# Local attention: inverse norms by ScalarE's logarithm and exponential, and a new order of VectorE's work in a tile

## The reference

```python
qkv = h @ wqkv
q, k, v = jnp.split(qkv, 3, axis=-1)          # 8 heads of 64 each
q = l2norm(q) * qs                            # each head's row divided by its norm
k = l2norm(k) * ksc
q, k = rotary_xpos(q, k)                      # a rotation with position-dependent scales
bk, bv = (look_around(bk), look_around(bv))   # a window's keys and those of the window before
sim = jnp.einsum('bhwid,bhwjd->bhwij', bq, bk)
sim = jnp.where(mask, -jnp.finfo(sim.dtype).max, sim)
attn = jax.nn.softmax(sim, axis=-1)
out = jnp.einsum('bhwij,bhwjd->bhwid', attn, bv)
x = x + o @ wo
```

## Time and profile before

| | us |
|---|---|
| median of 3 runs | 2674.88 (2674.61 to 2675.52) |
| profiled execution | 2674.28 |
| its span, first to last instruction | 2672.5 |
| PE / DVE / ACT / POOL busy | 2413.3 / 2081.4 / 1452.3 / 1173.9 |
| granted TensorE clock, mean | 0.963 of full speed |

### The profile page before, as it was taken

The page is one execution under the profiler, slowest core; times in us unless marked ns, Lnnn a source line. Parts: engine busy times, 40 slices in busy tenths (PEclk is TensorE's granted clock), DMA queues, the critical chain, the costliest instruction groups (busy, mean ns, idle before and its releaser), DMA issues.

```text
span 2672.5 us, 41317 instructions
## 1 busy us (share of the span) xinstructions
PE 2413.3 (90%) x14910; PEld 1127.4 (42%) x14910; DVE 2081.4 (78%) x3341; ACT 1452.3 (54%) x2541; POOL 1173.9 (44%) x980
## 2 busy tenths in 40 slices
PE   6799985988868977887699999999999999999897
PEld 5444434453335654565433333433343334333344
DVE  7798876428879965996588899888889988889642
ACT  5576652627647753675365555455545554555462
POOL 2211110306835531553056666566656665566630
PEclk9899988999989999999899999999999999999999
DMA  5000001010000000000100000000000000000000
GB/s 211 1 1 1 1 1 56 1 44 1 32 16 1 2 32 1 1 1 17 44 1 9 9 9 5 9 9 10 9 9 6 9 9 9 10 9 9 5 1 16
DMA packets 21128, 42.00 MB, mean 16 GB/s; under 512 B 10494, under 2 KB 12670, under 8 KB 19772
## 3 DMA queue, kind: packets, MB, share of 16 engines
q1 hardware_dynamic: 20924, 39.35, 4.3%
HBM read 34.90 MB, written 4.45 MB: 15 GB/s over the span
## 4 chain that ended last, share of the span: by engine, by line
PE 66%; DVE 23%; issue 6%; ACT 3%; POOL 1%; DMA 0%; DVEq 0%; POOLq 0%; ACTq 0%; SPq 0%
PE PS L2672 16%; PE PS L2663 15%; PE PS L1236 6%; PE PS L2635 5%; DVE WK L2188 2%; DVE NR L274 2%; DVE NR L2876 2%; PE PS L1218 2%; DVE WK L2164 2%; PE PS L680 2%; PE PS L682 2%; PE PS L681 2%; DVE WK L271 1%; DVE WK L2171 1%; PE PS L2618 1%
## 5 line engine op out<-in xcount | busy, mean ns | idle before, releaser
L2778 ACT ACTIVATE WK<-PS 128x1024 f32<-128x1024 f32 x512 | 497.6, 1022 | 458.1 <-PE PS L2663 452.4
L2955 POOL TENSOR_TENSOR W<-W,WK 128x512 f32<-128x512 f32 x448 | 575.8, 1287 | 383.4 <-DVE W L2894 382.1
L2876 DVE TENSOR_REDUCE NR<-PS 128x2 f32<-128x1024 f32 x512 | 625.3, 1223 | 131.7 <-PE PS L2636 115.9
L2672 PE MATMUL PS<-WK,W 128*64 128x512 f32 x2048 | 494.1, 603 | 0.0
L2663 PE MATMUL PS<-WK 64*128 64x512 f16 (+1 forms) x4096 | 484.0, 376 | 0.6 <-issue 0.6
L2894 DVE TENSOR_TENSOR W<-W,WK 128x512 f32<-128x512 f32 x448 | 342.8, 767 | 9.9 <-ACT WK L2778 9.4
L2663 PEld LDWEIGHTS PS<-WK 64*128 64x128 f16 (+1 forms) x4096 | 199.2, 94 | 219.8 <-ACT WK L2778 6.5
L2672 PEld LDWEIGHTS PS<-WK,W 128*64 128x64 f32 x2048 | 124.1, 136 | 246.9 <-issue 168.9
L2635 PE MATMUL PS<-WK 64*128 64x512 f16 x512 | 195.4, 382 | 5.5 <-DVE NR L2876 4.9
L2636 PE MATMUL PS<-WK 64*128 64x512 f16 x512 | 195.4, 382 | 0.0
L2203 POOL TENSOR_TENSOR WK<-WK,W 128x512 f32<-128x512 f32 x64 | 113.3, 1792 | 176.1 <-DVE WK L2148 93.8
(11 more groups left out here) (371 smaller groups left out, 4326.7 us busy)
## 6 DMA issues: line engine op xcount, KB each, us to landing
XB<-l_rdens SPq DMA_DIRECT2D x62, 128.0 KB, 2.9
W<-in_mw SPq DMA_DIRECT2D x8, 512.0 KB, 11.8
W<-in_l2w SPq DMA_DIRECT2D x1, 3114.0 KB, 12.0
W<-in_f1w SPq DMA_DIRECT2D x1, 2816.0 KB, 18.6
W<-in_l3w SPq DMA_DIRECT2D x1, 2816.0 KB, 9.9
W<-in_f3w SPq DMA_DIRECT2D x1, 2816.0 KB, 9.8
W<-in_mw SPq DMA_DIRECT2D x8, 256.0 KB, 12.3
la_second_tables<-W SPq DMA_DIRECT2D x1, 2048.0 KB, 6.3
```

What stands on the lines that cost most here:

```text
L2672: m = e.matmul(k.PS[64 * i:64 * i + 64, 4, :], self.V[:, kt, g, :], self.PTB[kt // 2 % 2][:, kt % 2, i, :], start=kt == 0, stop=kt == NT - 1)
L2778: e.activation(self.PTB[kt // 2 % 2][:, kt % 2, :, :], self.k.PS[:, 2 * (kt % 2):2 * (kt % 2) + 2, :], ACT.Exp, scale=1.0 / 64).then_inc(s ...
L2876: e.tensor_reduce(self.PM[ji % 2][:, u // 4, :, u % 4], self.k.PS[:, bk:bk + 2, :], AX.X, ALU.max).then_inc(self.maxes.sem)
L2955: e.tensor_tensor(ac, ac, p, ALU.add).then_inc(self.acc1.sem)
```

## The change

The inverse norm of tile t is no longer worked out by VectorE alone. VectorE sums the squares and clamps them (`dve_squares`), ScalarE takes the logarithm of the clamped sum into a new buffer LS and the exponential of minus one half of it into RS (`act_norms`), and VectorE makes one step of Newton's on RS (`rsqrt_step`). On VectorE the sum of squares of tile i is now made in round i between the two largest scores of tile i-2, a round earlier than before. The sum of the rotation, the Newton step and the scaling of tile i-1 (`dve_rotate`) stand ahead of both largest scores, and the reciprocals stand in front of the addition to X. ScalarE makes the squares ahead of the first exponentials instead of between the two, and loads the table that holds both functions at the start of the layer. TensorE's and GpSimd's code is as it was.

```diff
@@ -264,19 +264,25 @@
 def rsqrt(k, e, o, v, n, slot, step, at):
-    a, b = k.NR[:, 0, slot:slot + n], k.NR[:, 1, slot:slot + n]
+    a = k.NR[:, 0, slot:slot + n]
     e.wait_ge(*step(at))
     e.tensor_single_scalar(a.bitcast(I32), v.bitcast(I32), 1, ALU.logical_shift_right).then_inc(step.sem)
     e.wait_ge(*step(at + 1))
     e.tensor_scalar(o.bitcast(I32), a.bitcast(I32), -1.0, 1597463007.0, ALU.mult, ALU.add).then_inc(step.sem)
     for r in range(3):
         e.wait_ge(*step(at + 2 + 3 * r))
-        e.tensor_tensor(a, o, o, ALU.mult).then_inc(step.sem)
-        e.wait_ge(*step(at + 3 + 3 * r))
-        e.scalar_tensor_tensor(out=b, in0=a, scalar=-0.5, in1=v, op0=ALU.mult, op1=ALU.mult).then_inc(step.sem)
-        e.wait_ge(*step(at + 4 + 3 * r))
-        e.scalar_tensor_tensor(out=o, in0=b, scalar=1.5, in1=o, op0=ALU.add, op1=ALU.mult).then_inc(step.sem)
+        rsqrt_step(k, e, o, v, n, slot, step, at + 2 + 3 * r)
     return at + 11
+
+
+def rsqrt_step(k, e, o, v, n, slot, step, at):
+
+    a, b = k.NR[:, 0, slot:slot + n], k.NR[:, 1, slot:slot + n]
+    e.tensor_tensor(a, o, o, ALU.mult).then_inc(step.sem)
+    e.wait_ge(*step(at + 1))
+    e.scalar_tensor_tensor(out=b, in0=a, scalar=-0.5, in1=v, op0=ALU.mult, op1=ALU.mult).then_inc(step.sem)
+    e.wait_ge(*step(at + 2))
+    e.scalar_tensor_tensor(out=o, in0=b, scalar=1.5, in1=o, op0=ALU.add, op1=ALU.mult).then_inc(step.sem)
 class LayerNorm:
@@ -1843,7 +1849,7 @@
-    STEPS = 13
+    STEPS = 5
     def __init__(self, k, ld, l, tables, before=None):
         self.k, self.ld, self.l, self.begin, self.before = k, ld, l, Barrier(k), before
@@ -1867,7 +1873,7 @@
         self.PX = [heads(take(1536), 8) for _ in range(2)]
         self.PT = heads(take(1536), 8)
         self.OTT = take(512)
-        self.SS, self.RS = take(32)[:, 0:16], take(32)[:, 0:16]
+        self.SS, self.RS, self.LS = take(32)[:, 0:16], take(32)[:, 0:16], take(32)[:, 0:16]
         self.NM = [take(8) for _ in range(2)]
         self.DEN = [heads(take(16), 2) for _ in range(2)]
         self.kept = k.counter("x_kept", 16) if l == 0 else None
@@ -1879,6 +1885,8 @@
         self.v = k.counter("la_v", 16)
         self.sq = k.counter("la_squares", 16)
         self.step = k.counter("la_norm_steps", 16 * self.STEPS)
+        self.log = k.counter("la_norm_logs", 16)
+        self.inv = k.counter("la_norm_inverses", 16)
         self.sin = k.counter("la_sines", 32)
         self.cos = k.counter("la_cosines", 16)
         self.rotsum = k.counter("la_rotated", 16)
@@ -2032,6 +2040,7 @@
         m.then_inc(self.pv.sem)
     def act(self, e):
+        e.preload_act_table_set("natural_log_exp_and_others")
         self.begin.meet(e)
         if self.before:
             self.before.act_scale(e)
@@ -2046,12 +2055,14 @@
                 self.act_values(e, i)
             if 4 <= i:
                 self.act_turn_probs(e, i - 4, 1)
+            if i < NT:
+                self.act_squares(e, i)
             if 2 <= i < NT + 2:
                 self.act_exp(e, i - 2, 0)
             if 4 <= i:
                 self.act_weigh(e, i)
             if i < NT:
-                self.act_squares(e, i)
+                self.act_norms(e, i)
             if 2 <= i < NT + 2:
                 self.act_exp(e, i - 2, 1)
             if 1 <= i <= NT:
@@ -2075,6 +2086,17 @@
             e.wait_ge(*self.step(self.STEPS * (t - 1) + 1))
         e.wait_ge(*self.qk(t + 1))
         e.activation(self.SQ, self.QK[t % 2], ACT.Square).then_inc(self.sq.sem)
+
+    def act_norms(self, e, t):
+
+        if t:
+            e.wait_ge(*self.inv(t))
+        e.wait_ge(*self.step(self.STEPS * t + 2))
+        e.activation(self.LS, self.SS, ACT.Ln).then_inc(self.log.sem)
+        if t:
+            e.wait_ge(*self.rot(t))
+        e.wait_ge(*self.log(t + 1))
+        e.activation(self.RS, self.LS, ACT.Exp, scale=-0.5).then_inc(self.inv.sem)
     def act_turn_heads(self, e, t):
         k = self.k
@@ -2130,29 +2152,20 @@
         for i in range(NT + 5):
             if 1 <= i <= NT:
                 self.dve_cosines(e, i - 1)
-                self.dve_squares(e, i - 1)
+            if 3 <= i < NT + 3:
+                den = self.DEN[(i - 3) % 2]
+                e.wait_ge(*self.exp(2 * (i - 3) + 2))
+                e.reciprocal(den[:, 1, :], den[:, 0, :]).then_inc(self.rden.sem)
             if 5 <= i:
                 t = i - 5
                 e.wait_ge(*self.out(t + 1))
                 e.tensor_tensor(k.X[:, t, :], k.X[:, t, :], k.bank(6 + i % 2, 128), ALU.add).then_inc(self.added.sem)
-            if 3 <= i < NT + 3:
-                den = self.DEN[(i - 3) % 2]
-                e.wait_ge(*self.exp(2 * (i - 3) + 2))
-                e.reciprocal(den[:, 1, :], den[:, 0, :]).then_inc(self.rden.sem)
             if 1 <= i <= NT:
-                self.dve_norms(e, i - 1)
-            if 1 <= i <= NT:
-                ro = self.RO[(i - 1) % 2]
-                e.wait_ge(*self.sin(2 * i))
-                e.wait_ge(*self.cos(i))
-                e.tensor_tensor(ro, ro, self.PB, ALU.add).then_inc(self.rotsum.sem)
+                self.dve_rotate(e, i - 1)
             if 2 <= i < NT + 2:
                 self.dve_top(e, i - 2, 0)
-            if 1 <= i <= NT:
-                r4 = ro.rearrange("p (h d) -> p h d", h=16)
-                e.wait_ge(*self.rotsum(i))
-                e.wait_ge(*self.step(self.STEPS * i))
-                e.tensor_tensor(r4, r4, self.RS.unsqueeze(2).broadcast_to([P, 16, 64]), ALU.mult).then_inc(self.rot.sem)
+            if i < NT:
+                self.dve_squares(e, i)
             if 2 <= i < NT + 2:
                 self.dve_top(e, i - 2, 1)
@@ -2169,15 +2182,21 @@
         if t:
             e.wait_ge(*self.step(self.STEPS * t))
         e.tensor_reduce(self.SS, self.SQ.rearrange("p (h d) -> p h d", h=16), AX.X, ALU.add).then_inc(self.step.sem)
-
-    def dve_norms(self, e, t):
-
-        k, step, at = self.k, self.step, self.STEPS * t
-        if t:
-            e.wait_ge(*self.rot(t))
-        e.wait_ge(*step(at + 1))
-        e.tensor_scalar(self.SS, self.SS, 1e-24, None, ALU.max).then_inc(step.sem)
-        rsqrt(k, e, self.RS, self.SS, 16, 32, step, at + 2)
+        e.wait_ge(*self.step(self.STEPS * t + 1))
+        e.tensor_scalar(self.SS, self.SS, 1e-24, None, ALU.max).then_inc(self.step.sem)
+
+    def dve_rotate(self, e, t):
+
+        ro = self.RO[t % 2]
+        r4 = ro.rearrange("p (h d) -> p h d", h=16)
+        e.wait_ge(*self.sin(2 * t + 2))
+        e.wait_ge(*self.cos(t + 1))
+        e.tensor_tensor(ro, ro, self.PB, ALU.add).then_inc(self.rotsum.sem)
+        e.wait_ge(*self.inv(t + 1))
+        rsqrt_step(self.k, e, self.RS, self.SS, 16, 32, self.step, self.STEPS * t + 2)
+        e.wait_ge(*self.rotsum(t + 1))
+        e.wait_ge(*self.step(self.STEPS * (t + 1)))
+        e.tensor_tensor(r4, r4, self.RS.unsqueeze(2).broadcast_to([P, 16, 64]), ALU.mult).then_inc(self.rot.sem)
     def dve_top(self, e, t, hg):
         lo = 0 if t else 64
```

## The result

| | before | after |
|---|---|---|
| median | 2674.74 us (4 runs, 2674.39 to 2675.52) | 2700.25 us (4 runs, 2697.89 to 2703.08) |
| profiled execution, its span | 2674.28, 2672.5 us | 2702.12, 2700.3 us |
| PE / DVE / ACT / POOL busy | 2413.3 / 2081.4 / 1452.3 / 1173.9 | 2433.2 / 2072.8 / 1465.8 / 1168.2 |

The changed kernel takes 1.0095 of the time before (95% interval 1.0078 to 1.0113): slower by 25.5 us, where 28 were forecast.

A forecast was written before the change was run, and what follows sets the result against it. VectorE was taken as the bound, 97% busy in a layer's middle, TensorE next. Eleven rounds at 13.4 us give +15.4; with start and end +14.1 a layer, +28 in all: 2703 us, 8 in 10 within 2672 to 2718.

The forecast's parts named there:

- GpSimd's four instructions: Two multiplications of probabilities and two sine products, 5.3 us a round, all forecast to come in ahead of the scaling.
- The chain: One round from the start of the reciprocals to the next reciprocals, through GpSimd, scaling and ScalarE's exponentials: 13.4 us.
- the pair on the probabilities: GpSimd's two multiplications of probabilities after the reciprocals: 2.92 us, the sum of the rotation between them 1.08.
- the products: GpSimd's two sine products for the next tile, among VectorE's short Newton instructions: 1.19 us each.
- the two norms on ScalarE: Logarithm and exponential of 16 columns between the copy of the weighed values and half 1's exponentials: 0.40 us.
- step 3: Last of VectorE's three short Newton instructions before the scaling: passes in 0.06 us after one GpSimd instruction.
- this shift: If the sum of the rotation is issued before GpSimd, everything moves one place; the fourth GpSimd instruction precedes the scaling.
- The middle: Eleven rounds of a layer, each going from 11.98 to 13.4 us: +15.4 us.
- Start and end: A layer's first four tiles' cosines: -1.1 us; its last part, bound by TensorE: 0 to 1 less.
- The new wait: VectorE's reciprocals wait for the exponentials of half 1: 1.1 us a round.
- the second and third Newton step take no part in the exclusion: Rival: the second product falls beside the largest scores, a round of 12.1 us, 2674 to 2678 in all; chance 0.12.
- the third rival: TensorE's clock falls in its idle time and uncovered matmuls lose 0.8 us a round: 2722 us; chance 0.06.

The follow-up runs named there:

- moving one line: The changed kernel with the reciprocals moved behind the scaling, in front of the first largest scores: 2638.63 us, 0.9853 of the kernel before.
- The kernel before with the one move: The kernel before the change with only the reciprocals moved behind the scaling, ahead of half 1's largest scores: 2662.85 us, 0.9949 of the kernel before.
- the move on ScalarE: The changed kernel with ScalarE's logarithm and exponential for the norms moved behind the exponentials of half 1: 2691.84 us, 1.0054 of the kernel before.

## Why the prediction was right

The time, the side and the mechanism came out as forecast: GpSimd's four instructions all come in ahead of the scaling, between the short steps, and the loop closes through the exponentials. The sizes of two terms did not: the round was forecast 0.35 us too long, and the starts and ends came out dearer. Part of the closeness is chance.

- **The chain.** From the reciprocals to GpSimd's first instruction 0.28 us (forecast 0.27). To the end of the pair on the probabilities 4.24 (879.20 to 883.44; forecast 4.27). To the end of the products 6.71 (885.91; forecast 6.83 with the third step). From the largest scores to the next reciprocals 5.32 (873.88 to 879.20; forecast 5.41), the two norms on ScalarE 0.45 in it (forecast 0.40). The round is 13.05 and not 13.4, 0.05 below the range given for it: 0.09 in the part on ScalarE, and 0.26 ahead of the largest scores (7.73 against 7.99). There the sum of the rotation started before GpSimd, so the fourth of GpSimd's instructions went ahead of the scaling and not of step 3. The two products took 2.51 us and the forecast gave them 2.38, but the steps between added nothing where it gave them 0.06 each: 0.12 less up to the end of the products. From there to the largest scores it was 1.02 and not 1.16. The text had named this shift and not priced it; at most it was worth these 0.26.
- **The middle.** Eleven rounds: +11.7 and +11.5 us, forecast +15.4.
- **Start and end.** Forecast -1.1 and 0 to -1 a layer. In the first layer 2.77 us go to the squares ahead of the first cosines (from the first projection 4.67 before, 7.44 after), 2.5 come back in the start, 1.6 at the end: -1.3. In the second layer 4.35 go there (3.18 before, 7.53 after), 2.0 and 0.6 come back: +1.7. Part of that is the clock and not the change: the layer's first projections ran at 1.00 of full speed before and at 0.61 after.
- **The sum.** The first layer costs 10.4 us, the second 13.2, forecast 14.1 each. The two profiled executions differ by 27.8 because 4.5 more arose ahead of the layer; that this comes so near to 28 is chance. In the two faster runs of the changed kernel the difference is 23.4. So the change costs about 23 to 26 us, and 28 was 10 to 20% too much.
- **The new wait** is there with 1.04 us a round (11.4 in eleven), forecast 1.1.
- **The signs.** The round, the steps, the wait for the exponentials and GpSimd's one block are as foretold, or within 0.05 us. Two signs are missed: the sum of the rotation took 1.22 us and not 2.5, since it went before GpSimd, and TensorE waited 1.5 us a round and not 2.5. The first is the shift told above; TensorE's wait is not on the chain.
- **The rivals.** That the second and third Newton step take no part in the exclusion is refuted by their 1.39 and 1.20 us; the Trainium skill's rule of two SBUF inputs (SBUF — State Buffer, "SBUF: two separate sides"), by which whichever of the two engines starts first keeps the other out for the whole instruction, holds for 16 columns as well. The advice of moving work to ScalarE (the Trainium skill, Perfetto Trace Analysis, "Optimizing Scalar/DVE Operations") pointed at a gain, and taken by itself it was one: the new norms, which do so, took less than the old ones in both orders. It says nothing on the order, which decided here. The clock did fall in the middle, to 0.96 and 0.95, where TensorE is idle for 12% of the time; its busy time rose from 119.94 to 126.81 us. In the first layer's middle three rounds had a stretch at the lower level and took 13.05, 13.22 and 13.09 us where the others took about 13.03. So TensorE's slack covered nearly all of it, and the third rival's 0.8 us a round did not come; the share of time at the lower level that it took rests on no row.

What I did not see: that moving one line turns the loss into a gain. The forecast weighed what GpSimd would fall on, but not where else the reciprocals could stand.

## What to carry to other kernels

Where two engines exclude each other, what costs is not how much the one works but what stands in the other's queue when it is released: a chain of short dependent instructions behind the release lets one long foreign instruction in at every link, so three steps of 0.2 us took 4 us. Put the instruction that releases the other engine behind such a chain and ahead of work that does not exclude it; here that one line was worth 62 us, against 25 that the whole change cost, and 14 in the kernel before, where the cosines and two short steps still stood in GpSimd's way. When counting such a block, count the foreign engine's instructions, not their overlap in percent, and look at which engine bounds next: with TensorE at 10.9 us a round, the move on ScalarE that had been worth 8.4 us gained 3.6.

## What the runs showed of the hardware

- A VectorE instruction that starts 0.01 us ahead of GpSimd's goes first (879.47 against 879.48). In every round shown here in which both engines had such instructions waiting, they then went in turn, one of each, whatever their lengths (16 columns against 768).
- A scalar_tensor_tensor of 128x16 with two SBUF inputs is held up for a whole GpSimd instruction: 1.39 and 1.20 us in place of 0.17. So are 16-column instructions that read one buffer of SBUF: 1.44 and 1.39 us for the two steps of the guess, 0.64 for the clamp. The sum of squares is not: it kept its 1.21 us beside the sine products (879.13, with the reciprocals behind the scaling).
- A logarithm and an exponential of 128x16 take 0.23 and 0.22 us and put the next instruction off by 0.45. The trace has one load of their table for each of the two layers (1.28 us, L2043), none between the two functions.
- TensorE kept its full clock through eleven rounds when it was busy 119.38 of 119.54 us and also at 119.94 of 131.83, and was at 0.96 and 0.95 on average where it was idle for 16.7 of 143.52 us and 15.3 of 143.71. The kernel before with the one move had 0.99 at 123.81 of 128.12.
- A part that was not touched ran at the full clock in one execution and at half in another from 419 to 433 us, and came out about 4 us later.
